# Experts' weight loads released by the landing of an earlier scatter instead of by VectorE's splits

## The reference

```python
logits = xf @ w_cls.T                       # 32 experts + 32 that do nothing
scores = softmax(logits)
_, topk_idx = top_k(scores + bias, 8)
...
buf = zeros((E, CAP, H)).at[ids_s, pos].set(x_exp[order], mode='drop')   # E = 32, CAP = 256, H = 512
gu = einsum('ech,ehf->ecf', buf, w_gate_up)  # (32, 512, 512)
g, u = split(gu, 2, axis=-1)
y = einsum('eci,eih->ech', silu(g) * u, w_down)   # (32, 256, 512)
...
routed_out = einsum('tk,tkh->th', w_r, y_exp)
x = x + out
```

## Time and profile before

| | |
|---|---|
| median of 3 runs | 973.87 us |
| lowest and highest | 973.5 and 981.56 us |
| the profiled execution, its own time | 979.09 us |
| its span, first to last instruction | 977.3 us |
| mean granted TensorE clock (1 is full) | 0.979 |
| TensorE busy over the span | 902.5 us (92%) |
| VectorE, ScalarE, GpSimd busy | 772.9, 503.3, 482.5 us |
| waits of GpSimd's scatters for a landing, 765 to 977 us | 51.2 us in 24 |

### The profile page before, as it was taken

The page is one execution under the profiler, slowest core; times in us unless marked ns, Lnnn a source line. Parts: engine busy times, 40 slices in busy tenths (PEclk is TensorE's granted clock), DMA queues, the critical chain, the costliest instruction groups (busy, mean ns, idle before and its releaser), DMA issues. The chain is left out here.

```text
span 977.3 us, 14567 instructions
## 1 busy us (share of the span) xinstructions
PE 902.5 (92%) x4362; PEld 731.1 (75%) x4362; DVE 772.9 (79%) x1843; ACT 503.3 (51%) x867; POOL 482.5 (49%) x395
## 2 busy tenths in 40 slices
PE   4789999999999999999969999999976999998893
PEld 3577888888888888888848888888854677776672
DVE  6978888888888889888977777777776788887670
ACT  5455655555554655554563222332224687876671
POOL 2466766666766667766630000000006456775662
PEclk9999999999999999999999999999998999999897
DMA  8001111111111111110563676443155699999633
GB/s 309 6 33 49 51 46 50 59 45 49 39 59 50 44 59 51 39 59 35 195 224 145 209 266 208 148 148 119 56 192 185 162 331 323 293 299 279 201 43 43
DMA packets 67368, 127.06 MB, mean 130 GB/s; under 512 B 12072, under 2 KB 14504, under 8 KB 65232
## 3 DMA queue, kind: packets, MB, share of 16 engines
q1 hardware_dynamic: 58144, 114.67, 33.7%
q0 software_dynamic: 9136, 11.31, 6.2%
HBM read 106.53 MB, written 32.90 MB: 143 GB/s over the span
## 5 line engine op out<-in xcount | busy, mean ns | idle before, releaser
L595 POOL TENSOR_TENSOR a_t<-a_t 128x512 f32<-128x512 f32 x80 | 105.1, 1314 | 99.0 <-DVE a_t L358 99.0
L604 POOL TENSOR_TENSOR a_fQ<-a_fQ,a_den 128x512 f32<-128x512 f32 x64 | 88.0, 1375 | 71.8 <-DVE a_den L396 71.8
L213 PE MATMUL a_PQ<-w_h,a_xT_h 128*128 128x512 f32 x384 | 106.9, 400 | 10.1 <-DVE w_l L345 9.4
L782 PE MATMUL r_PY<-w_h,r_o_h 128*128 128x512 f32 x256 | 105.9, 414 | 3.4 <-DVE r_o_l L884 3.4
L1070 POOL TENSOR_SCALAR r_vr<-r_mv 128x1 f32<-128x1 f32 x16 | 8.4, 525 | 196.6 <-DVE r_mv L895 196.6
L213 PE MATMUL a_PQ<-w_l,a_xT_h 128*128 128x512 f32 x384 | 104.5, 395 | 0.0
L213 PE MATMUL a_PQ<-w_h,a_xT_l 128*128 128x512 f32 x384 | 103.4, 391 | 0.0
L782 PE MATMUL r_PY<-w_h,r_o_l 128*128 128x512 f32 x256 | 101.0, 395 | 0.0
L1223 POOL DMA_INDIRECT out<-m_y,si x39 | 69.1, 1772 | 64.5 <-DMA out<-m_y,si 51.2
L782 PE MATMUL r_PY<-w_l,r_o_h 128*128 128x512 f32 x256 | 100.5, 393 | 0.0
L392 DVE CUSTOM_DVE_ANT_0 a_m<-a_fQ,a_z 128x128 f32<-128x128 f32 x256 | 100.4, 445 | 0.0
(11 more groups left out here) (182 smaller groups left out, 2245.3 us busy)
## 6 DMA issues: line engine op xcount, KB each, us to landing
oT<-a_o SPq DMA_DIRECT2D x64, 256.0 KB, 2.4
v_l<-in_wgu SPq DMA_DIRECT2D x32, 512.0 KB
raw<-in_wgu SPq DMA_DIRECT2D x24, 512.0 KB
v_l<-oT SPq DMA_DIRECT2D x11, 1024.0 KB, 7.2
v_l<-in_wd SPq DMA_DIRECT2D x16, 512.0 KB
raw<-in_wd SPq DMA_DIRECT2D x12, 512.0 KB
v_h<-oT SPq DMA_DIRECT2D x5, 1024.0 KB, 6.9
out<-r_x SPq DMA_DIRECT2D x18, 256.0 KB, 2.0
```

Source lines behind the costliest of these rows:

```text
L213: last = eng.matmul(bank[:, :], a[:, k, :], w[:, 4 * i + k, :], start=s == 0 and k == 0, stop=s == 2 and k == 3)
L595: eng.tensor_tensor(t1[:, r % 2, :], t1[:, r % 2, :], t2[:, r % 2, :], ALU.add).then_inc(sm["xr"], 1)
L604: eng.tensor_tensor(q, q, den[:, n % 2, :].unsqueeze(2).broadcast_to([P, 4, P]), ALU.mult).then_inc(sm["fs"], 1)
L782: last = eng.matmul(PY[c % 2][:, :], a[:, c % 2, h * P:(h + 1) * P], b[:, h, :], start=h == 0 and s == 0, stop=h == NH - 1 and s == 2)
```

## The change

In the loop over the loads, the wait for `m_wl` goes. From expert 10 on, a wait for `m_s` takes its place, for a value that says that the scatter of expert e - 10 (and those before) has landed. The loads of experts 8 and 9 have neither. The waits for the last product of the buffer stay.

```diff
@@ -1192,7 +1192,8 @@
                     for part in range(3):
                         for t in range(2):
                             eng.wait_ge(sm[f"m_gu{t}" if part < 2 else f"m_yd{t}"], e - RING + 1)
-                        eng.wait_ge(sm["m_wl"], 3 * (e - RING + 3) + part + 1)
+                        if e >= RING + 2:
+                            eng.wait_ge(sm["m_s"], 32 * (e - RING - 1))
                         if part < 2:
                             load_up(sm, eng, ring, wgu, e, (part,))
                         else:
```

## The result

The changed kernel takes 1001.84 us (median of 4 runs, 1000.52 to 1002.40) against 977.62 us (973.5 to 981.56) before: a ratio of 1.0296, with a 95% interval of 1.0255 to 1.0337. It is 3% slower. The forecast was 969.9 us, the range 959 to 984, on the scale of the three runs with median 973.87; as a change it was -4.0 us, and +24.2 was measured. The profiled execution took 1002.01 us, 22.9 us more than the one of before.

The account below looks back on a forecast made before the run. The prediction took the serial chain of scatter landings on GpSimd as the bound. Its terms, -1.9 - 0.6 - 2.7 + 1.2 = -4.0 us, took the median of 973.87 to 969.9 us, range 959 to 984.

Parts of the forecast that it names:

- (a): Removed split wait: loads 8 and 9 start earlier, shortening the wait before expert 2's scatter: -1.9 us (0 to -3.8).
- (b): Added landing wait: loads 12 to 31 start up to 18 us later, in step with scatters; no cost by itself.
- (c): Load and scatter now start together: -0.6 us over 20 links, from meetings at experts 8 and 14 (-14 to +13).
- Rival 2: Links of experts 2 to 22: fresh burst before every scatter, +0.66 us each, 988 us; chance 0.16 with rival 4.
- rival 4: New wait comes later than the removed one; late loads could make ScalarE and TensorE wait; chance 0.16 with Rival 2.
- (d): Two-half scatters of 11, 15 and 18: exactly one load falls into each, so waits shrink: -2.7 us.
- (e): End of the loads: load 31 runs beside the scatter of 22, one more link with traffic: +1.2 us.
- Rival 1: Scatter chain unchanged: DMA near saturation, weight traffic still beside every scatter; 974 us; chance 0.22.
- Rival 3: Steady beat of loads takes 18 us off the chain, but TensorE limits the gain to about 11: 963 us; chance 0.20.

Follow-up runs that it names:

- e3_first_two: Changed kernel, but from expert 10 on loads wait for the split again, not the landing; only loads 8 and 9 are freed: 980.17 us, ratio 1.0010.
- e5_behind: Changed kernel, but from expert 10 on loads wait for a one-column GpSimd memset behind a scatter's issue, not the landing: 967.83 us, ratio 0.9922.
- e11_two_and_one: Changed kernel, but two thirds of each load are released behind the scatter's issue, the last third behind the two gathers: 966.09 us, ratio 0.9922.
- e10_after_gathers: Changed kernel, but each load is released in one piece behind the two gathers that follow a scatter: 982.74 us, ratio 1.0086.
- e4_behind: Changed kernel, but loads wait for a semaphore count placed after the scatter in GpSimd's program, not for the landing: 1004.20 us, ratio 1.0209.

## Why the prediction was wrong

What bounds the kernel was right: the chain of scatters sets the end. The chain from the scatter of expert 2 to that of 23 took 143.9 us (784.95 to 928.88) and now takes 168.8 (782.94 to 951.76); the chain behind it is the same, 40.30 and 40.25 us. With 2.0 us that expert 2 starts earlier, 24.9 - 2.0 is the 22.9 us between the two profiled executions.

(a) -1.9 us for the freed loads 8 and 9: not borne out, and not settled by time (e3_first_two, 1.0010 with 0.4% on either side, which takes in both 0 and -1.9 us). In the changed kernel's trace the gain is absent: the wait before expert 2 was 4.41 us, not shorter than the 4.12 of before. Load 8 did start at 749.59, as said, but the third part of load 9 (771.78) and the first two of load 10 (772.25) went out on either side of the start of expert 1's scatter (772.11), so that scatter was not freed of traffic.

(b) was right in its conclusion. The new condition is the later one, loads 12 to 31 keep step with the scatters, and no split waited. Its size was low, since the scatters that release the loads fell back as well: load 28 went out at 920.60 and load 31 at 943.64, 34 and 31 us later than before and not up to 18.

(c) is the step that failed: "their mean, 1.43, is what a link costs now, so I take -0.6 us", and its bounds of -14 and +13 us. The 17 links behind a single scatter waited 3.06 us each on average instead of 1.46, which is 27.2 us. Rival 2 named the place and the mechanism, but its price of 0.66 us was too low by more than half; I gave it, with rival 4, 0.16. Two things were misread. First, the meeting at expert 8 was not the new order. The third part of that load came 5.4 us after the first two, as this row of the kernel before shows:

```profile
829.34 0.37 SPq L1090 DMA_DIRECT2D raw<-in_wd  x1
```

so 1.05 MB stood in front there, and 1.57 MB does now. Second, I averaged two meetings that lie on different sides of the scatter's start. The load of expert 25 at +0.35 us and that of 18 at -0.12 us are no two samples of one state: the cost depends on the order, as e5_behind against the changed kernel shows (1.9 us of delay, 34 us of time). The row nearest in order was the one with 2.12 us alone. The start of the scatter's issue is not the divide, though: the one load of the changed kernel that went out 0.12 us behind it (expert 14) was followed by a wait of 3.84 us. What a whole load costs between 0.2 and 1.7 us behind the start was not tried; the meeting at +0.35 us, like that at -0.12, had its third part 5.4 us late.

(d) -2.7 us for two-half scatters: measured +3.7 (the waits behind 11, 15 and 18 are 4.39, 2.19 and 3.33, 9.91 us in all, against 6.23). The -2.7 us was half of a bound, and no row showed a second half that was clear of its load; none was.

(e) +1.2 us: measured 2.85 (the scatter of 23 waits 3.15 us where it waited 0.30). The place was right, the size was that of (c).

The waits so grew by 27.2 + 3.7 + 2.85 = 33.7 us, and the chain by 24.9: 8.8 us came back in shorter issues. A scatter's issue takes 1.62 us on average instead of 1.85, a gather's 1.22 instead of 1.30, and there are 24 and 42 of them. I had not looked at that; why they are shorter was not tried.

Rival 1 (nothing changes while a load is beside every scatter) is refuted by the DMA share, 0.78 in place of 0.94: the traffic did not stay dense. Rival 3 named the gain that was to be had and where TensorE would limit it (963 us), but the change was not its cause; e5_behind and e11_two_and_one come to 968 and 966 us by the opposite order. Rival 4 did not come true.

What stays open: why SP's queue can hold GpSimd's packets back for most of a burst. That the scatter's own packets were ready soon after its issue's end rests on the scatters without a load, whose first packet moves 0.6 us after the issue's end; for a scatter with a load it is not visible. A kernel without weight traffic, which would give the chain's floor, wasn't tried.

## What to carry to other kernels

When two queues share the DMA engines and one of them is in a serial chain, release the bulk transfer by an event behind the issue of the critical one, not by the event that starts both: here 2 us of order were worth 3.4% of the kernel. The release must not come too late either: behind the gathers (e10_after_gathers) the load met the next scatter, and by the ratios the kernel was 1.7% slower than with the release behind the scatter. The release that tied the load to the chain's landing also left the engines empty between links (1.1 us in the link of expert 9), and the DMA share fell from 0.94 to 0.78 while the stretch with loads grew from 145 to 173 us. And before an experiment on order is judged, check in the trace that the order is the one that was meant.

## What was not expected of the hardware

A load that was released by a semaphore count behind a DMA issue in GpSimd's program went out 0.13 us before that issue began (e4_behind), although the issue takes 1.5 us; the end of a small memset behind it came 1.6 us after its start, 0.1 us after its end (e5_behind). A scatter that meets no load moves its first packet 2.0 us after its issue's start, and one with a load issued 0.2 us in front after 5.0 us. The kernel before spreads by 1.0 to 1.8% from run to run in groups of 15 to 19 runs (971.85 to 989.56 us in the widest); chance meetings of its loads and scatters would explain that, but it was not tried. Of the kernels that fix the order, the changed one spreads by 0.2% and e5_behind by 0.3%, but e11_two_and_one by 0.8%.
